# A four-layer kernel on Trainium2: one half's projection, norm, queries and first top-16 scores moved into the last units of a local attention

## The reference, cut to what matters

```python
def _self_attn(h, w_qkv, b_qkv, w_so, b_so):
    qkv = jnp.roll(h @ w_qkv + b_qkv, -SHIFT, axis=1)
    qkv = qkv.reshape(B, nw, WIN, 3, H, D)
    q, k, v = (qkv[:, :, :, 0], qkv[:, :, :, 1], qkv[:, :, :, 2])
    scores = jnp.einsum('bnqhd,bnkhd->bnhqk', q, k) / jnp.sqrt(D)
    attn = jax.nn.softmax(scores, axis=-1)
    o = jnp.einsum('bnhqk,bnkhd->bnqhd', attn, v).reshape(B, L, C)
    return jnp.roll(o, SHIFT, axis=1) @ w_so + b_so

def _topk_cross_attn(h, ctx, w_q, b_q, w_kv, b_kv, w_co, b_co):
    q = (h @ w_q + b_q).reshape(B, L, H, D)
    ...
    scores = jnp.einsum('bqhd,bkhd->bhqk', q, k) / jnp.sqrt(D)
    top_s, top_i = jax.lax.top_k(scores, TOPK)          # TOPK = 16 of 64
    attn = jax.nn.softmax(top_s, axis=-1)
    ...
    return o @ w_co + b_co

x = x + _self_attn(_ln(x) * (1 + sc_msa) + sh_msa, ...) * g_msa
x = x + _topk_cross_attn(_ln(x) * (1 + sc_mca) + sh_mca, context, ...) * g_mca
x = x + _swiglu(_ln(x) * (1 + sc_mlp) + sh_mlp, ...) * g_mlp
```

## Time and profile before

| | us |
|---|---|
| median of 3 runs | 1672.08 (1668.72 to 1673.46) |
| the profiled execution, its time | 1674.23 |
| its span, first to last instruction | 1672.4 |
| PE busy | 1528.8 (91%) |
| DVE busy | 1049.2 (63%) |
| ACT busy | 769.9 (46%) |
| POOL busy | 379.4 (23%) |
| mean granted clock of PE | 0.968 of 2.4 GHz |

### The profile page before, as it was taken

The page is one execution under the profiler, slowest core; times in us unless marked ns, Lnnn a source line. Parts: engine busy times, 40 slices in busy tenths (PEclk is TensorE's granted clock), DMA queues, the critical chain, the costliest instruction groups (busy, mean ns, idle before and its releaser), DMA issues.

```text
span 1672.4 us, 26374 instructions
## 1 busy us (share of the span) xinstructions
PE 1528.8 (91%) x10485; PEld 927.8 (55%) x10485; DVE 1049.2 (63%) x2946; ACT 769.9 (46%) x1228; POOL 379.4 (23%) x419
## 2 busy tenths in 40 slices
PE   5899998999998999878998999899999899887898
PEld 3456574444354857556764666543444476655676
DVE  3564344999727445899457334399991744579953
ACT  1315421588853533325543533138886354333444
POOL 3510005343016000114133000344400701001320
PEclk9898999999999999999999999899999999999999
DMA  9400007221020000000130000542202000000000
GB/s 337 140 1 0 0 22 161 37 39 31 2 76 1 1 1 2 2 1 2 32 133 1 0 1 1 143 66 40 40 2 77 1 1 1 3 1 1 1 1 25
DMA packets 37551, 59.60 MB, mean 36 GB/s; under 512 B 7360, under 2 KB 26980, under 8 KB 36532
## 3 DMA queue, kind: packets, MB, share of 16 engines
q1 hardware_dynamic: 25239, 34.71, 6.3%
q0 software_dynamic: 9408, 15.85, 6.1%
q10 hardware_dynamic: 2780, 7.36, 1.2%
HBM read 42.03 MB, written 2.10 MB: 26 GB/s over the span
## 4 chain that ended last, share of the span: by engine, by line
PE 68%; DVE 19%; issue 6%; ACT 5%; DMA 1%; POOL 1%; ACTq 0%; DVEq 0%; POOLq 0%
PE ps L993 9%; PE ps L1005 8%; PE ps L464 7%; PE ps L1299 4%; PE ps L978 3%; PE ps L870 3%; PE ps L1092 3%; DVE taken L2351 3%; PE ps L1100 3%; DVE rs L2036 2%; PE ps L848 2%; PE ps L592 2%; DVE mxw L2028 2%; PE ps L600 2%; PE ps L1156 2%
## 5 line engine op out<-in xcount | busy, mean ns | idle before, releaser
L2221 DVE TENSOR_REDUCE mm<-ps 128x1 f32<-128x1024 f32 x256 | 310.2, 1223 | 32.9 <-PE ps L978 25.6
L1618 ACT ACTIVATE pt<-ps 128x512 f32<-128x512 f32 x512 | 276.8, 599 | 59.1 <-PE ps L993 41.3
L2464 POOL TENSOR_TENSOR rstd<-ve,minus_half 128x4 f32<-128x4 f32 x32 | 35.7, 1116 | 748.8 <-DVE ve L1900 748.8
L993 PE MATMUL ps<-qx,kx 64*128 64x512 f32 x512 | 188.3, 445 | 1.0 <-ACT pt L1618 1.0
L978 PE MATMUL ps<-kx,qx 48*128 48x512 f32 x512 | 186.6, 444 | 0.2
L1005 PE MATMUL ps<-pt,v 128*32 128x256 f32 x2048 | 158.7, 390 | 0.0
L993 PEld LDWEIGHTS ps<-qx,kx 64*128 64x128 f32 x512 | 78.9, 184 | 95.9 <-ACT pt L1618 85.9
L2111 DVE TENSOR_TENSOR rlo<-ring,rhi 128x512 fp32r<-128x512 f32 x48 | 33.2, 692 | 114.5 <-ACT ring L1569 114.4
L1005 PEld LDWEIGHTS ps<-pt,v 128*32 128x32 f32 x2048 | 42.9, 108 | 85.6 <-ACT pt L1618 61.7
L978 PEld LDWEIGHTS ps<-kx,qx 48*128 48x128 f32 x512 | 75.4, 184 | 22.0 <-issue 18.0
L592 PE MATMUL ps<-filler 128*128 128x512 f32 x262 | 83.6, 434 | 0.0
(11 more groups left out here) (374 smaller groups left out, 3396.1 us busy)
## 6 DMA issues: line engine op xcount, KB each, us to landing
wm<-in_L_xcond_W_mlp_dram SPq DMA_DIRECT2D x4, 1024.0 KB, 7.9
qx<-q_hi POOLq DMA_DIRECT2D x64, 64.0 KB, 2.6
kx<-k_hi POOLq DMA_DIRECT2D x64, 64.0 KB, 2.8
w3a<-in_L_xcond_w_m_dram SPq DMA_DIRECT2D x2, 2048.0 KB, 8.1
w<-in_L_xcond_e_w_dram SPq DMA_DIRECT2D x6, 512.0 KB, 7.8
w<-in_L_xcond_e_w_dram SPq DMA_DIRECT2D x2, 1536.0 KB, 13.3
s_ada<-in_L_xcond_w_ada_dram ACTq DMA_DIRECT2D x1, 2304.0 KB, 23.0
qx<-q_lo POOLq DMA_DIRECT2D x32, 64.0 KB, 2.6
```

Of the source, the lines that this page charges most:

```text
L993: pe.matmul(ps[:, bank, :], kx[r, p % 4, kc * P:(kc + 1) * P], qx[r, p % 4, half * 512:(half + 1) * 512], start=True, stop=True).then_inc( ...
L1618: act.activation(pt[:, u % 8, half * 512:(half + 1) * 512], ps[:, bank, :], ACT.Exp, scale=QK_SCALE).then_inc(st_read, 1)
L2221: return dve.tensor_reduce(mm[:, p % 2, e, t:t + 1], place(), X, ALU.max).then_inc(ring_read, 1)
```

## The change

All of it is order, but for the buffers of the searches, which are counted from another start (tile t now uses slot (t + 2) % 3 of `prob3`). The same instructions run, and 10 more fillers per batch in front of the second projection, 8 after it as before. The lines in the changed file are 3 to 5 higher on DVE and ACT; `top_scores` is L1212 there.

```diff
                     if u + 9 < N_UNIT:
                         window_tokens(u + 9, 0)
+                    if u == 9:
+                        projection(R_B_SA, 0, wso, oT, 0, (None, (wo_ready, u0 + N_UNIT // 2), None))
                     if u:
                         window_values(u - 1)
...
-                    elif u == 9:
-                        projection(R_B_SA, 0, wso, oT, 0, (None, (wo_ready, u0 + N_UNIT // 2), None))
+                    elif u == 11:
+                        ln(6, 0, bank=0)
+                    elif u == 12:
+                        query(2, 0, 14, wq3, bank=0)
                     elif u == 13:
-                        ln(6, 0, bank=0)
-                query(2, 0, 14, wq3, bank=0)
+                        top_scores(0)
                 window_values(N_UNIT - 1)
...
-                top_scores(0)
+                top_scores(1)
+                keep_busy(6, 10)
                 projection(R_B_SA, 1, wso, oT, 4, (None, (wo_ready, u0 + N_UNIT), None))
-                top_scores(1)
-                keep_busy(3, 8)
-                ln(6, 1)
-                query(2, 1, 14, wq3)
+                top_scores(2)
+                keep_busy(6, 8)
                 for t in range(TB):
...
                     top_turn(t)
+                    top_values(t)
                     if t == 0:
-                        top_scores(2)
-                    top_values(t)
+                        ln(6, 1)
+                        query(2, 1, 14, wq3)
...
@@ ACT @@
+                    elif u == 11:
+                        ln(6, 0, (mod, M3_SC_CA, M3_SH_CA), 0)
+                    elif u == 12:
+                        query(2, 0, C_BQ3C, 0)
                     elif u == 13:
-                        ln(6, 0, (mod, M3_SC_CA, M3_SH_CA), 0)
-                query(2, 0, C_BQ3C, 0)
+                        top_copy(0)
...
-                top_copy(0)
                 top_copy(1)
                 exp(0)
+                top_copy(2)
+                turned(0)
                 ln(6, 1, (mod, M3_SC_CA, M3_SH_CA))
                 query(2, 1, C_BQ3C)
-                turned(0)
-                top_copy(2)
...
@@ DVE @@
-                for u in range(N_UNIT):
+                for u in range(N_UNIT - 2):
                     if u + 9 < N_UNIT:
                         window_maximum(u + 9)
+                    if u == 9:
+                        link(residual(5, 0, 0))
+                        statistics(b, 6, 0)
                     if u:
                         window_divide(u - 1)
-                    if u == 10:
-                        link(residual(5, 0, 0))
-                        statistics(b, 6, 0)
-                    elif u == 11:
+                    if u == 8:
+                        build_keys(2)
+                    elif u == 10:
                         normalise(b, 6, 0)
-                    elif u == 13:
-                        build_keys(2)
-                window_divide(N_UNIT - 1)
...
                     best(t)
...
+                    elif t == 0:
+                        window_divide(N_UNIT - 3)
+                    elif t == 1:
+                        normalise(b, 6, 1)
                     mark(t)
                     if t == 0:
-                        link(residual(5, 1))
-                        statistics(b, 6, 1)
+                        window_divide(N_UNIT - 2)
+                        window_divide(N_UNIT - 1)
...
                     next_best(t)
-                    if t == 0:
-                        normalise(b, 6, 1)
...
                     mask(t)
+                    if t == 0:
+                        link(residual(5, 1))
+                        statistics(b, 6, 1)
```

More of the change, by code:

```diff
@@ L1199, in window_values, with top_scores @@
                     ins.then_inc(wpv_done, 1)
+                t0 = b * T
+                def top_scores(t):
+                    if t % TB == 0:
+                        pe.wait_ge(qT_ready, b * 2 * N_Q + 4 + t // TB + 1)
+                    if t == 0:
+                        pe.wait_ge(kblk_ready, b + 1)
+                    else:
+                        pe.wait_ge(ts_read, t0 + t)
+                    for c in range(KC):
+                        ins = pe.matmul(ps[:, c, :], qT[:, t // TB, c, t % TB * P:(t % TB + 1) * P],
+                                        kblk[:, c, :, :].rearrange("p h s -> p (h s)"), start=True, stop=True)
+                    ins.then_inc(ts_ready, 1)
                 window_linear(0, 0)
@@ L1266, in top_turn @@
                         for j in range(4):
[L1267 removed]
+                            ins = pe.transpose(ps[:, 2 + half, j * P:(j + 1) * P], prob3[:, (t + 2) % 3, (4 * half + j) * P:(4 * half + j + 1) * P], ident[:, :])
                         ins.then_inc(tp_turned, 1)
@@ L1710, in window_exp, with top_copy @@
                     act.activation(wprobT[:, u % 2, :, :].rearrange("p (r o) q -> p r (o q)", o=2), ps[:, 4:8, 0:2 * P], ACT.Exp, scale=QK_SCALE).then_inc(wp_exp, 1)
+                t0 = b * T
+                def top_copy(t):
+                    act.wait_ge(ts_ready, t0 + t + 1)
+                    if t >= 3:
+                        act.wait_ge(tp_turned, 2 * t0 + 2 * t - 4)
+                    act.activation(prob3[:, (t + 2) % 3, :], ps[:, 0:2, :].rearrange("p a n -> p (a n)"), ACT.Copy).then_inc(ts_read, 1)
                 window_queries_keys(1)
```

28 lines of the change are left out of this document (5 added, 23 removed).

## The result

The changed kernel takes **1677.68 us** (median of 12 runs, 1675.57 to 1680.57) against 1672.91 us for the kernel before on the same chip (12 runs, 1668.72 to 1681.19): a recorded ratio of 1.0024, 95% interval 1.0013 to 1.0036 (the two medians alone would give 1.0029). It is a little slower; the forecast was 1667.2 us. The profiled execution of the changed kernel has a span of 1675.6 us and a time of 1677.42; before it was 1672.4 and 1674.23. The spans differ by 3.2 us.

What follows compares the result with a forecast made beforehand. The searches were taken as one DVE-bound stretch whose end moves with its start and its work. Per batch 5.65 - 3.65 + 0.45 = 2.45 us, 4.9 for two: median 1672.08 to 1667.2 us, range 1664 to 1672.5.

Steps and rivals of the forecast that it cites:

- Term 1: Start of the searches: the first MAX8 comes 5.65 us earlier per batch.
- Term 2: DVE's search stretch: three local-attention divisions (units 13 to 15) move into it, costing 3.65 us per batch.
- Term 3: DVE's waits before the second tile's mask: 0.75 us shrinks to 0.1 to 0.3, gaining about 0.45 per batch, assuming full clock.
- the first rival: Second half's query stays at half clock, the change gives nothing: 1672 to 1673 us; chance 0.17, shared with a late start.
- The slower rival: Half clock from the second half's transposes through `top_scores(3)`: mask(1) 3.4 us later than before, 1679 us; chance 0.06.

Runs made afterwards that it cites:

- e1: Changed kernel with 11 more fillers per batch around the first tile's values, the second half's transposes and its query: 1671.56 us, ratio 0.9984 to the kernel before.
- e2: Changed kernel with the second tile's exponential ahead of the eviction of the first tile's output on ACT: 1672.40 us, ratio 0.9991 to the kernel before.
- e10: Changed kernel with eight more fillers at the start of the evidence stage, near 924 us: 1673.64 us, ratio 0.9999 to the kernel before.
- e11: The kernel of e9 with eight more fillers at the start of the evidence stage, near 924 us: 1668.19 us, ratio 0.9960 to the kernel before.
- e9: Changed kernel with e2's swap and the division of tile 5 moved behind `mark_next(6)`: 1672.48 us, ratio 0.9986 to the kernel before.
- e14: The kernel of e9 with eleven fillers in the feed-forward's own gaps: 1663.16 us, ratio 0.9934 to the kernel before.
- e13: Changed kernel with eleven fillers in the feed-forward's own gaps: 1671.53 us, ratio 0.9985 to the kernel before.
- e3: The kernel before with 13 fillers (about 3.0 us) behind the first batch's searches as pure delay: 1676.15 us, ratio 1.0009 to the kernel before.
- e4: Changed kernel with 2 fillers (0.45 us) behind the first batch's searches as delay: 1677.55 us, ratio 1.0021 to the kernel before.
- e5: Changed kernel with 6 fillers (1.4 us) behind the first batch's searches as delay: 1678.87 us, ratio 1.0026 to the kernel before.
- e12: The kernel before with eight more fillers at the start of the evidence stage, near 924 us: 1676.43 us, ratio 1.0010 to the kernel before.
- e7: The kernel before with 18 more fillers ahead of the second half's transposes, for a full-clock query: 1681.57 us, ratio 1.0050 to the kernel before.

## Why the prediction was wrong

**Term 1 was right.** 5.65 us earlier forecast, 21.37 - 15.72 = 5.65 measured.

**Term 2 was right.** The three divisions took DVE 3.7 us in all (1.28 for the first, 2.39 for the other two) against 3.65. The second projection was there in time: no wait in front of the residual, as forecast.

**Term 3 failed.** It took full clock at the second half's query and a gain of 0.45 us. The clock was at 0.50 for most of the query's 5.43 us, and the wait for the exponential grew to 2.5 us, where the waits of 0.75 were to shrink to 0.1 to 0.3. First MAX8 to third took 716.28 - 681.04 = 35.24 us instead of 33.0: Term 3 was a loss of 1.7 us a batch (2.45 of wait instead of 0.75) and not a gain of 0.45. What is left of the sum is 5.65 - 3.7 - 1.7 = 0.3 at the third MAX8 and 0.15 at the last mask. For the searches this is the first rival, half clock at the query and nothing gained. The failed step was the reading of one row: 740 to 742, 0.56 busy of 2.00 at clock 1.00, as a sign that such gaps leave the clock alone. That row shows a stretch in which the clock had not fallen; it doesn't show that it wouldn't with more such gaps next to it. The same trace of before held two places that say so. Eight us further on, at 749.9 us, the clock had fallen behind gaps of 1.77, 1.61, 0.74 and 1.33 us, and in the first batch's feed-forward it fell at 541.6 us, after gaps of 1.39 and 0.96 us and ahead of the end of one of 1.63. PE's rows of before ahead of 749.9 us, and the clock behind it:

```profile
737.80 0.44 PE L1281 MATMUL ps<-ident,o_tok 128*128 128x128 f32 x2 [1.77 <-DVE o_tok L2017]
742.17 1.09 PE L1267 MATMUL ps<-ident,prob 128*128 128x128 f32 x8 [1.61 <-DVE prob L2369]
744.00 2.00 PE L1274 MATMUL ps<-vx,probT 128*128 128x64 f32 x16 [0.74 <-ACT probT L1740]
748.31 0.44 PE L1281 MATMUL ps<-ident,o_tok 128*128 128x128 f32 x2 [1.33 <-DVE o_tok L2017]
```

```profile
750.00:753.00 3.00, 3.00 (x9) 2.37 (x8) 2.97 (x31) 0.50 (x1) 0.00 (x0) 0.50 0.00 0
```

e1 (fillers) and e2 (query off the path) give back 2.25 and 2.4 us per batch at the third MAX8, so the term and its size are shown. The Trainium skill, TensorE: Matmul & The Clock Gate, in its section on a second HAM failure mode, says of a kernel that cycles through PSUM banks that frequent small gaps between groups of matmuls are enough to make the clock swing between its two levels. This trace agrees, with gaps of 0.74 to 1.16 us. Half clock should have had more than the 0.17 that it got.

**The sum had a silent term.** I took all that lies outside the searches as fixed. It is not: it ran 10.2 us more at half clock (34.1 against 23.9) and took 3.69 us more. With Term 3 put right the gain is still not the forecast's 4.9 us: e1's searches are 1.5 and 2.5 us shorter than before's, and its ratio of 0.9984 is a gain of 2.7 us, with an interval that reaches 1. The slower rival (half clock from the transposes through the scores) named the right kind of loss in the wrong place: it had the searches 3.4 us longer in each batch, and they became 0.15 shorter. That its 1679 us lies near the measured 1677.68 is luck.

**Where the 3.69 us went.** The two first traces, each from its own first exp, show it as a sum. At the last mask of the first batch after is 0.15 us ahead. By the transposes of the third layer's cross-attention, 632 us behind the exp, it is 0.79 behind. There before meets 3.4 us of half clock (at 1299.4 us) and after doesn't. Before, then after:

```profile
1297.67 1.41 PE L600 MATMUL ps<-ident,xhat 128*128 128x128 f32 x8 [1.23 <-DVE xhat L1907]
1299.77 5.20 PE L464 MATMUL ps<-hT,wqc 128*128 128x512 f32 x8 [0.69 <-ACT hT L1472]
```

```profile
1298.30 1.41 PE L600 MATMUL ps<-ident,xhat 128*128 128x128 f32 x8 [1.23 <-DVE xhat L1912]
1300.39 3.70 PE L464 MATMUL ps<-hT,wqc 128*128 128x512 f32 x8 [0.69 <-ACT hT L1475]
```

So after wins 1.50 us on before and begins the feed-forward 0.71 us ahead. On the passage it meets the half clock, loses 4.25 us, and ends 3.54 behind. Outside the passage both have the same amount of half clock between the searches (23.9 us), in other places.

How far this is shown: that the passage costs 4.25 us more when the clock falls in the feed-forward's gaps, with the same work, is shown, and so is that fillers in these gaps keep the clock up (six passages of six). The distance came down by 3.3 to 3.5 us with fillers ahead of the feed-forward (e10, e11; its start moved 0.8 to 0.9 us later) and with fillers in its gaps in e9's kernel (e14). In the changed kernel itself fillers in the gaps did not bring it down (e13), and e3 and e4 have the long distance without the fall. So the feed-forward is where after's traces lose the time, and not shown to be the only place where such a kernel can lose it. Before meets the same fall in its first batch, so it is no cost of the new order as such; in the second batch the traces tie it to the time at which the stage begins. Why the clock falls at one place and not at another is not settled, and delays did not steer it (e3 to e5). Also open is why e13 lost time in and behind its first searches, and with it why the change is not faster even with the fillers.

## What to carry to other kernels

Before taking one stretch of a trace as a sign that the clock stays up, look through the same trace for stretches with like gaps in which it fell: here there were two.

Where PE is the bound and its work has gaps near one microsecond, add up the time outside the edited stretch too, by its half-clock time in the records: a local gain can be paid back hundreds of microseconds later, and a local edit should be judged by the same two events on both sides of it as well as by the total.

Try to fill the gaps of a PE-bound stage with matmuls that end before the wait does (here eleven fillers, no delay, 0.34% on their own) before tuning the order of other engines. Fillers one stage earlier are no sure means: those near 924 us left the half clock there as it was, helped two kernels by moving a later stage (e10, e11), and had nothing to give back in the third, whose clock had not fallen in that stage (e12). And a filler pays only as far as another engine was waiting for what it speeds up (e7).

## What the runs showed of the hardware that was not expected

- The distance between the two batches' exps took few values. In 18 of 19 traces it is within 0.25 us of 798.8, 802.2, 805.5 or 808.9, although the searches ran from 3.3 us shorter to 2.4 us longer than before's and up to 3 us of delay was added. Half clock between the searches is 20.5 us at the first value, 23.9 to 30.7 at the second, 27.3 to 34.1 at the third, 34.1 to 41.0 at the last. e13, at 806.59, is the exception.
- A microsecond at half clock cost less than half a microsecond here: 3.69 us for 10.2 between after and before (0.36 each), 4.25 for 10.2 in the passage through the feed-forward (0.42), 1.50 for 3.4 at 1299 us (0.44).
- At the same gaps (1.38, 0.96 and 1.62 to 1.64 us) and the same matmuls the granted clock was 1.00 or 0.52, with a start 0.7 us apart (behind the exp).
- The same work from the start to the first batch's exp took from 659.59 to 666.27 us in thirteen traces.
